# An attention and expert kernel: the channel sums are added to the band on GpSimd, and three transfers change place on the load queue

## The reference

```python
xn = _layernorm(x)
# attention, per batch and head
q = (xn @ Wq + bq) * SCALING;  k = xn @ Wk + bk;  v = xn @ Wv + bv
w = q @ k.T + rel_to_abs(q @ emb_rel_k.T)      # rel term only for |t - s| <= 4
p = softmax(w)
a = p @ v + abs_to_rel(p) @ emb_rel_v
# experts: top 2 of 8 per row
h = silu(xn @ w1[e]) * (xn @ w3[e]);  y = sum_e share[e] * (h @ w2[e])
out = x + (a @ Wo + bo) + y
```

## Time and profile before

| | |
|---|---|
| median of 3 runs | 2143.64 us (2141.66 to 2147.24) |
| the profiled execution | 2146.0 us, its span 2144.1 us |
| PE busy | 1800.1 us, 84% of the span |
| DVE busy | 1506.6 us, 70% |
| ACT busy | 1103.0 us, 51% |
| POOL busy | 773.5 us, 36% |
| DMA | 395.56 MB, mean 184 GB/s |

### The profile page before, as it was taken

How to read it: one execution, slowest core, us unless ns; L and a number is a source line. 1 busy time by engine, 2 the same in 40 slices (tenths; PEclk the granted TensorE clock), 3 DMA queues, 4 the chain that set the end, 5 groups by cost and what they waited for, 6 DMA issues and landing times. The chain is left out here.

```text
span 2144.1 us, 36132 instructions
## 1 busy us (share of the span) xinstructions
PE 1800.1 (84%) x11121; PEld 1026.0 (48%) x11121; DVE 1506.6 (70%) x2627; ACT 1103.0 (51%) x2115; POOL 773.5 (36%) x529
## 2 busy tenths in 40 slices
PE   6992328888888889899988859999999999999992
PEld 4761002222222223233322227777777777778882
DVE  3765677666666667777766239888888888898552
ACT  3541005565666566566688854444445454445550
POOL 1002899755444544400000013534444354443111
PEclk9985559999999999999999979999999999999996
DMA  5998997555543344233455156776767677675655
GB/s 181 344 347 269 250 295 208 156 134 138 143 128 104 104 137 101 77 79 69 110 165 176 40 202 224 228 228 214 247 210 237 211 231 232 212 251 168 201 166 166
DMA packets 227567, 395.56 MB, mean 184 GB/s; under 512 B 15440, under 2 KB 161760, under 8 KB 219296
## 3 DMA queue, kind: packets, MB, share of 16 engines
q1 hardware_dynamic: 193088, 279.97, 43.5%
q0 software_dynamic: 25824, 93.73, 14.3%
q10 hardware_dynamic: 8576, 20.97, 2.7%
HBM read 306.37 MB, written 87.99 MB: 184 GB/s over the span
## 5 line engine op out<-in xcount | busy, mean ns | idle before, releaser
L736 DVE CUSTOM_DVE_ANT_0 t_seen<-t_s,hide 128x1024 bf16<-128x1024 f32 x512 | 603.4, 1221 | 285.8 <-PE t_s L623 282.4
L804 ACT ACTIVATE t_pr<-t_s 128x512 f32<-128x512 f32 x1024 | 560.6, 604 | 329.2 <-PE t_s L636 231.5
L632 PE MATMUL t_s<-t_q,t_k 98*128 98x512 bf16 x1024 | 366.2, 392 | 95.6 <-DMA t_q<-t_mt 63.6
L623 PE MATMUL t_s<-t_k,t_q 96*128 96x512 bf16 x1024 | 331.5, 407 | 97.5 <-DVE t_mx L736 71.7
L1349 ACT ACTIVATE e_sg<-e_pa,e_down 128x256 f32<-128x256 f32 x312 | 148.0, 474 | 424.5 <-PE e_pa L1224 412.4
L1420 DVE SCALAR_TENSOR_TENSOR e_wl<-e_ws,e_up,e_wh 128x512 f16<-128x512 f32 x312 | 320.0, 1038 | 13.6 <-ACT e_wh L1310 0.5
L1233 PE MATMUL e_py<-e_w2s,e_hT 128*128 128x256 f32 x1248 | 324.3, 383 | 1.0 <-DVE e_hT L1442 1.0
L632 PEld LDWEIGHTS t_s<-t_q,t_k 98*128 98x128 bf16 x1024 | 97.8, 98 | 437.4 <-ACT t_pr L804 260.5
L1224 PE MATMUL e_pa<-e_xh,e_wh 128*128 128x256 f16 x1248 | 239.4, 274 | 49.0 <-DVE e_xl L1412 41.9
L647 PE MATMUL t_po<-t_pr,t_vx 128*32 128x512 f32 x2048 | 279.7, 619 | 0.7 <-ACT t_pr L804 0.7
L1224 PE MATMUL e_pa<-e_xh,e_wl 128*128 128x256 f16 x1248 | 238.7, 273 | 0.0
(11 more groups left out here) (202 smaller groups left out, 1857.5 us busy)
## 6 DMA issues: line engine op xcount, KB each, us to landing
e_ws<-in_L_ffn_w_dram SPq DMA_DIRECT2D x78, 1024.0 KB, 4.9
e_w2s<-in_L_ffn_w_dram SPq DMA_DIRECT2D x39, 1024.0 KB
e_vs<-v_rows POOLq DMA_DIRECT2D x32, 1152.0 KB, 5.8
t_kw<-k_rows POOLq DMA_DIRECT2D x22, 1152.0 KB
t_q<-q_stack SPq DMA_DIRECT2D x32, 768.0 KB, 6.1
t_k<-k_stack SPq DMA_DIRECT2D x32, 768.0 KB, 9.0
t_kw<-in_L_ffn_w_dram ACTq DMA_DIRECT2D x16, 1024.0 KB, 4.9
t_kw<-k_rows SPq DMA_DIRECT2D x10, 1152.0 KB, 7.3
```

The source lines that it names most:

```text
L623: last = nc.tensor.matmul(s1[:, buf, half * CH:(half + 1) * CH], q1[0:ROWS, u, h, i * P:(i + 1) * P], k1[0:ROWS, u, h, half * CH:(half + 1 ...
L632: last = nc.tensor.matmul(s2[:, bank, :], k2[0:ROWS + MROWS, u, h, i * P:(i + 1) * P], q2[0:ROWS + MROWS, u, h, half * CH:(half + 1) * CH] ...
L736: nc.vector.tensor_tensor_reduce(out=seen[:, buf, :], in0=s1[:, buf, :], in1=c["hide"][:, (TB - 1 - i) * P:(TB - 1 - i) * P + L], scale=1. ...
L804: nc.scalar.activation(pr[:, k % BP, n % HG], s2[:, turn(u, n)], ACT.Exp).then_inc(exp_ok, 1)
```

## The change

Three things change, all in `attention`.

- GpSimd adds `dot` to `band` itself, behind the last fold of each window, and waits for that add before its next window. `dot` has one buffer; the wait for VectorE is gone. VectorE keeps only the maximum over the distances. For group 0 it takes all eight of these behind its 32 maxima.
- In `step`, `maximum(g + 1, ...)` stands ahead of `load1(g + 3, ...)` where it stood behind it.
- The 13 fills leave the loop that loads windows 2 to 9. They are issued behind the first maximum rows and the two loads that follow them. The fill of `expert_sums` (4325 KB) goes behind step 1.

```diff
-                sp.wait_ge(zero_ok, 2)
                 for t in range(2, TB + 2):
                     sp.wait_ge(sum_ok, t - 1)
                     load_window(sp, t, t % 2, win_early)
-                    for z in range((t - 2) * N_ZERO // TB, (t - 1) * N_ZERO // TB):
-                        sp.dma_start(zeros[z], zero[:].broadcast_to([P, 6, XE])).then_inc(zero_out, 16)
-                sums = dr["moe"].rearrange("(n p) e -> p n e", p=P)
-                sp.dma_start(sums, zero[:, :, 0:E].broadcast_to([P, NT + 1, E])).then_inc(sums_out, 16)
                 maximum(0, 0)
                 load2(1, 0, 1, 1)
                 def step(g, b2, g2, u, more1=True, more2=True):
+                    maximum(g + 1, 1 - u)
                     if more1:
                         sp.wait_ge(s1_ok, X1 * (g + 2))
                         load1(g + 3, 1 - u)
-                    maximum(g + 1, 1 - u)
...
                 load1(2, 0)
+                sp.wait_ge(zero_ok, 2)
+                for z in range(N_ZERO):
+                    sp.dma_start(zeros[z], zero[:].broadcast_to([P, 6, XE])).then_inc(zero_out, 16)
                 step(0, 0, 2, 0)
                 step(1, 0, 3, 1)
+                sums = dr["moe"].rearrange("(n p) e -> p n e", p=P)
+                sp.dma_start(sums, zero[:, :, 0:E].broadcast_to([P, NT + 1, E])).then_inc(sums_out, 16)
...
# GpSimd, window_products
-                            after(pool, band_ok, t - 1)
-                            nc.gpsimd.tensor_tensor(dot[:, u, :].rearrange("p (q o) -> p q o", o=1), terms[:, :, 0:w],
+                            nc.gpsimd.tensor_tensor(dot[:].rearrange("p (q o) -> p q o", o=1), terms[:, :, 0:w],
                                                     terms[:, :, w:2 * w], ALU.add).then_inc(sum_ok, 1)
+                    pool.wait_ge(sum_ok, t + 1)
+                    scores = band[:, t, :, :].rearrange("p m h -> p (m h)")
+                    nc.gpsimd.tensor_tensor(scores, scores, dot[:], ALU.add).then_inc(band_ok, 1)
                     if more:
-                        pool.wait_ge(sum_ok, t + 1)
                         load_window(pool, t + 2, u, win_in)
+                    pool.wait_ge(band_ok, t + 1)
...
# VectorE
-                def window(t, u, piece):
-                    if piece == 0:
-                        dve.wait_ge(sum_ok, t + 1)
-                        scores = band[:, t, :, :].rearrange("p m h -> p (m h)")
-                        nc.vector.tensor_tensor(scores, scores, dot[:, u, :], ALU.add).then_inc(band_ok, 1)
-                    else:
-                        dve.wait_ge(band_ok, t + 1)
-                        nc.vector.tensor_reduce(bmax[:, t, :], ...
+                def window(t):
+                    dve.wait_ge(band_ok, t + 1)
+                    nc.vector.tensor_reduce(bmax[:, t, :], ...
...
-                        if g0 and n % HG >= HG - PIECES:
-                            window(n // HG, n // HG % 2, n % HG - (HG - PIECES))
-                        elif more and not g0 and n in range(8, 8 + 2 * PIECES, 2):
-                            window(TB * (b + 1) + 2 * v, 0, (n - 8) // 2)
+                        if more and not g0 and n == 8:
+                            window(TB * (b + 1) + 2 * v)
...
+                    if g0:
+                        for t in range(TB):
+                            window(t)
```

More of the change, by code:

```diff
@@ L408, in attention @@
     XS = 2 * TB * HG
-    PIECES, FOLDS = 2, 4
+    FOLDS = 4
     HF = XS // X
@@ L442, in attention @@
         kw = sb("kw", [P, 2, NM * E])
-        dot = sb("dot", [P, 2, NM * H])
+        dot = sb("dot", [P, NM * H])
         xn_in, sent, zero_ok, zero_out = sems("xn_in"), sems("sent"), sem("zero_ok"), sem("zero_out")
@@ L708, in _ @@
                 neg_v = neg[:].rearrange("p (b i) (g h) -> p b g h i", i=TB, h=HG)
-                def window(t, u, piece):
-                    if piece == 0:
-                        dve.wait_ge(sum_ok, t + 1)
-                        scores = band[:, t, :, :].rearrange("p m h -> p (m h)")
-                        nc.vector.tensor_tensor(scores, scores, dot[:, u, :], ALU.add).then_inc(band_ok, 1)
-                    else:
-                        dve.wait_ge(band_ok, t + 1)
-                        nc.vector.tensor_reduce(bmax[:, t, :], band[:, t, :, :].rearrange("p m h -> p h m"),
-                                                AX.X, ALU.max).then_inc(bmax_ok, 1)
+                def window(t):
+                    dve.wait_ge(band_ok, t + 1)
+                    nc.vector.tensor_reduce(bmax[:, t, :], band[:, t, :, :].rearrange("p m h -> p h m"),
+                                            AX.X, ALU.max).then_inc(bmax_ok, 1)
                 def maxima(b, v):
@@ L747, in maxima @@
                     if g0:
-                        for piece in range(PIECES):
-                            window(TB, 0, piece)
+                        window(TB)
                     if more:
-                        for piece in range(PIECES):
-                            window(TB * (b + 1) + 2 * v + 1, 1, piece)
+                        window(TB * (b + 1) + 2 * v + 1)
                 nc.vector.memset(mparts[:], 0.0).then_inc(zeros_ok, 1)
```

## The result

The changed kernel takes 2168.02 us (median of 4 runs, 2160.89 to 2176.37). The kernel before, run on the same chip, takes 2145.44 (4 runs, 2141.66 to 2148.57). The ratio is 1.0107, with a 95% interval of 1.0062 to 1.0153: the change makes the kernel 22.6 us slower. The forecast was 2152, slower, with a range of 2133 to 2175. The direction and the range hold; the size was a good third of the measured one, and 2168 lies outside the 2142 to 2163 to which the forecast itself gave 0.47.

A forecast was written before the change was run, and what follows sets the result against it. TensorE was taken as the bound, stopped about 5 us a group by late maximum rows. From the profiled 2146.0, +48 (fills) - 58 (rows first) + 19 (GpSimd free) gave 2155, stated as 2152 us in the metric, range 2133 to 2175.

The forecast's parts named there:

- Windows and the first chain: In front of group 0: a window takes 11.0 us, the chain ends 2.6 us later, TensorE begins group 0 near 316.
- The fills: Behind the first maximum rows: fills complete near 367, holding GpSimd's first scatter, window 9 and VectorE; group 1 begins 48 us late.
- Maximum rows ahead of load1: In SP's queue: nine periods fall from 59.5 us to the floor and small later waits go, a return of 58 us.
- Rival B: GpSimd's window loads, no longer tied to VectorE, lie on the maximum rows: return 31 instead of 58, 2176 us; chance 0.12.
- The floor: TensorE's period for a group without row waits, taken as 53.2 us from the 53.3 between groups 10 and 11.
- GpSimd set free: Groups 2 to 7: free GpSimd holds up VectorE's chain, 13 us plus 2 for clock; loads meeting rows 4; together 19.

## Why the prediction was right or wrong

**Windows and the first chain: right.** A window takes 11.05 us (289.80 to 300.85) where 11.0 was forecast; the add takes 0.49, so the value between the bounds was well taken. The chain ended 1.2 us later than before, forecast 2.6. TensorE began group 0 at 313.61, forecast 316.

**The fills: right, and proven apart.** The scatter was forecast at T = 367 and started at 367.10; VectorE's first maximum at 381.1, measured 380.78. Group 1 began 51 us late in its first step by the trace (forecast 48). The fills alone cost 52.5 us in time, and taking the scatters away from the fills returned 45 of them by the ratios (1.0107 to 0.9898).

**Maximum rows ahead of load1: the amount was near, its cause was not.** The forecast gave the whole return of 58 to the order in SP's queue, and that step failed: the order alone brings 18. The runs showed two causes with one wait in common. Rows first alone brings 18 us, the adds alone 19, the kernel with both 23, and rows first with GpSimd's load moved away 65. Rival B named this second cause, but with the wrong sign: it took GpSimd's loads to lie on the rows once they are *no longer* tied to VectorE. The tie itself put them there. My argument against it, "with load1 ahead and no GpSimd it is still 1.3 us", compared with the wrong thing; groups 10 to 12 had `load1` in front of the rows just as groups 1 to 9 had, and a wait of 1.3 and not 6. That row said that most of the wait was GpSimd's.

The floor was wrong too: a period without a wait takes 52.0 us and not 53.2, since the 53.3 I read it from held a wait of 1.30, which I did not take off: without it that row says 52.0. That is 9 x 1.2 = 11 us more return than forecast.

**GpSimd set free: right in kind, a little small.** L738, L739 and L742 were held in three groups, and those periods cost 8.9, 8.4 and 6.1 us over 52, together 23.4, forecast 15 + 4. The changed kernel's runs lie 15.5 us apart, those of the two kernels that hold GpSimd until the chain has ended 1.5 and 5.3; that the draw of the collisions differs by run is the likely reason, and no second profile shows it.

**Not in the forecast:** ScalarE's wait at group 8 (8 us), and 3.7 us from the first step of group 13 to the end (1068.3 us against 1064.6), which no run explains and which stay open; in the ten other profiles this part takes 1064.1 to 1067.4.

**The sum.** In the profiled execution +3 for the fills, -11 for the floor, +8 for ScalarE, +4.4 for the collisions, +3.7 at the end is +8.1 beyond the forecast; it came out at 2163.55 against 2155, so +8.5. The profiled run lies 4.5 us under the median of its four. So the terms that missed are the return of the row order and what GpSimd set free costs, -39 net: it is -23 to -27 in the kernel with the fills back, and -34 in the profiled execution of the changed kernel (17.4 in all, less the 51.1 of group 0). That the total still fell into the range owes something to luck. The 58 was one cause with the right amount for two, the floor erred by 11 us one way, and the collisions, ScalarE's wait and the end erred by 16 the other.

## What to carry to other kernels

When a small transfer is late, look at every queue, not only at what stands ahead of it in its own: here a load of 1.3 MB in GpSimd's queue, released just behind the instruction that releases the rows, cost more than the stacked load ahead of them (42 us against 18, in this order; the wait moved with `load1` still ahead was not run). Where two engines depend on each other, the wait's place in the program chooses what the freed engine does next, and so what its load and its memory traffic fall on; moving one wait past four instructions was worth 42 us, while moving the work itself was worth 19. And before a fill or another low-priority transfer is put later, follow its first reader's program downward: one scatter at the head of GpSimd's queue stopped three engines for over 50 us.

## What the runs showed of the hardware

- A VectorE instruction of 128x32 that starts beside a GpSimd multiply or fold ends with it, and then the next one can be held by GpSimd's next: 4.65, 2.60 and 1.28 us in a row at 301.30, against 0.21, 0.18 and 0.21. L715 (at most 0.42) and the row maxima, which read PSUM (1.2), were held in none of the twelve profiles. L740 (0.19) was not held there, but it can be: in the kernel with the adds alone one took 5.63 us, with GpSimd's next multiply beginning at 552.80 and ending at 557.86.

```profile
552.29 5.63 DVE L740 SCALAR_TENSOR_TENSOR t_mparts<-t_mb,t_mparts 128x32 bf16<-128x32 f32 x1
```

- Two small rows (1.3 us to issue) reach TensorE in 2.8 us when the DMA engines are idle, and in 7.1 us when a load was issued in another queue 0.9 us ahead of them. TensorE's waits for them were 2.2 to 4.6 us a group. The prediction took from "Queues, rings and completion order" (DMA: Bandwidth & Descriptors, the Trainium skill) that a short transfer waits a turn of each engine, and concluded that the rows lose little. The same section makes a turn a whole packet of about 9 to 17 descriptors. GpSimd's load of the keys is 128 pieces of 9216 B, an estimated 8 for each of 16 engines, so one turn can be all of it. The measured wait agrees with the rule read in this way; the conclusion was wrong.
- Two loads of 0.79 MB issued right behind the rows made ScalarE wait 7.2 to 8.0 us at one place of its program, in all seven kernels that issue them there and in none of the other five.
